# Attention with relation maps: both sides of a unit in one ring of four map buffers, logarithm and inverse for two maps at a time, three units ahead

## The chip, the core and the metric

One core of a Trainium2 chip runs the whole kernel in one launch. The metric is the time of one execution on the device in microseconds (us). Before the change the median of three runs was 4457.25 us (4456.81 to 4464.74). The engines are TensorE (PE; PEld is its weight load), VectorE (DVE), ScalarE (ACT), GpSimd (POOL) and SyncE (SP), which issues most of the DMAs. Each runs its own instructions in order and meets the others through semaphores.

## What is computed

A pre-norm block over 4096 tokens of width 256: attention with 16 heads, and a mixture of 8 experts of which each token takes two. The change lies in the attention alone:

```python
x = hidden_states                       # layer-normed, 1 x 4096 x 256
q, k, v = (x @ W.T + b, split in 16 heads of 16)
attn_scores = einsum('bihd,bjhd->bhij', q, k) / scale
li = x @ rel_W[:, :d].T
lj = x @ rel_W[:, d:].T
logits = li[:, :, None, :] + lj[:, None, :, :] + rel_b      # 3 classes for each pair of tokens
relation_probs = softmax(logits, axis=-1)
bias = einsum('bijk,hk->bhij', relation_probs, logical_bias)
gate = sigmoid(x @ gate_W.T + gate_b)
attn_scores = attn_scores + gate * bias
out = softmax(attn_scores) @ v          # for each head
```

For each pair (query i, key j) three relation probabilities are needed. With the differences of the logits, d0 and d1, two of them follow from r = 1 / (1 + exp(d0) + exp(d1)) and its like: that is what a *map* holds here.

## The kernel before

Three stages follow one another: the projections (to about 188 us), the attention (`attend`, from there to about 3600 us) and the experts. Only `attend` changes.

**Chunks and steps.** The 4096 queries are taken in 32 chunks of 128. The first 24 chunks run in a loop on the chip of three turns with eight chunks each (`in_chunks`), the last eight stand behind it without a loop. A chunk goes over 32 key tiles of 128 keys, `jt` = 0 to 31; I call one of them a *step*. In a step PE does, in this order (L814 products, L802 relation, L833 maxima, L856 values):

- the scores of the *next* step, `pe_scores(jt + 1)`: 16 relation matmuls for the even heads, 16 for the odd heads, 32 products of queries and keys on top of them in the same two halves of the PSUM tensor `sc`. Each half may be overwritten only after ACT has read it, so the relation matmuls of a half wait for the exponentials of this step (`p_ready`);
- a pair of maximum matmuls (`pe_step_pair`, slot 0) for the row maxima of the next chunks;
- `pe_pv(jt)`: 16 matmuls, exponentials times values, into `acc`, when both exponentials of this step are done;
- a second pair of maximum matmuls (slot 1).

ACT does the two exponentials of the step's scores (L690) and then a piece of work on a relation map. DVE does four maximum reductions (L716), one for each maximum matmul, out of a ring of three PSUM banks (`mx`), and between the third and the fourth one *clamp* (L708, `dve_d`): the logit difference of a query row and 512 keys, capped at 43, for one of the two differences.

**Maps.** A *unit* is 512 keys, four steps; a chunk has 8 units. A unit has two maps, side 0 (the first 64 queries of the chunk) and side 1 (the others), on 128 partitions each, so 16 maps in a chunk, numbered `g`, with unit `u = g // 2`. The life of a map before the change:

1. DVE clamps both halves of it into `dl` (side, half), one in each step, `D_AHEAD` = 3 steps of clamping ahead of ACT's counting;
2. ACT exponentiates both halves at once, 1024 elements a row, from `dl` into `ex` (L668; even steps, `act_r_exp`);
3. POOL adds the two halves (L613);
4. ACT takes the logarithm of 1 + sum (L675) and the exponential of its negative (L677), 512 elements a row, in the next, odd step (`act_r_inv`);
5. POOL rounds the result to 16 bits (`rhi`, L623) and keeps the rest (`rlo`, L625);
6. SP sends both by six DMAs per unit into `rst`, the operand of the relation matmuls, which holds two units.

`ex` is a ring of two maps, `dl` another of two. The map worked on in step `jt` is `g = jt // 2 + R_AHEAD`, four maps (two units) ahead of the unit that PE uses. The order on each engine is written out by hand.

**Prologue of the stage.** PE and DVE go over 64 pairs of maxima for chunk 0 and 16 for chunk 1; during the first eight pairs DVE clamps the first four maps. SP meanwhile loads the key logits `dj`, eight DMAs of 512 KB (unit 0 and 1 count on semaphore `dj_in0`, units 2 to 7 on `dj_in1`), and behind them in its queue a store to `attention_out`. DVE waits for `dj_in1` after all pairs.

## Time and profile before

| what | value |
|---|---|
| median of three runs | 4457.25 us (4456.81 to 4464.74) |
| the profiled execution: its own time | 4429.6 us |
| its span, and granted TensorE clock | 4427.9 us, 0.943 |
| PE, PEld busy | 3634.5 us (82%), 2679.5 us (61%) |
| DVE busy | 3607.0 us (81%) |
| ACT busy | 3309.5 us (75%) |
| POOL busy | 1970.2 us (44%) |
| first score exponential of chunk 0 | at 341.52 us |
| last ones of chunk 31 | at 3594.52 us |

The span is cut by the page into 40 slices of 110.7 us, one digit each for the busy tenths:

```profile
PE   7548888888888888888888888989888864499991
DVE  4298999999899999998999999999999623377773
ACT  2008999999899999998999999999999941244440
POOL 0014444454444455544455454555555532533335
PEclk9759999999999999999999999999999986699996
```

Slices 4 to 33 are the attention's chunks. Busy shares of 80 to 90% on three engines at once say that they wait for one another in turn; what a piece of work is worth has to be read from the order in which they meet. Times of instructions below are in microseconds from the start of the span unless ns is written. Instructions of one engine overlap a little (the next one starts up to 0.1 us before the last ends), so the distance between starts is what counts for a sum.

### The profile page before, as it was taken

What the parts mean: (1) busy time and instruction counts of PE and PEld (TensorE: products, weight loads), DVE (VectorE), ACT (ScalarE), POOL (GpSimd) and SP (SyncE); (2) the same over time, 40 slices, a digit from 0 to 9 for tenths busy, and PEclk for the clock granted to TensorE, in tenths of its full rate; (3) what the DMA queues carried; (4) which work ended last, traced back from release to release, by engine and by line L of the source; (5) the groups of instructions that cost most, each with busy time, mean ns of one, the idle gap of its engine ahead of it and who ended that gap; (6) DMA issues with size and microseconds to landing.
All of it is one profiled execution on the core that took longest, in us unless ns stands there. A gap on an engine that the chain in (4) does not pass through costs nothing. (4 is left out here: it accounts for less than half of the span.)

```text
span 4427.9 us, 243862 instructions
## 1 busy us (share of the span) xinstructions
PE 3634.5 (82%) x106896; PEld 2679.5 (61%) x106896; DVE 3607.0 (81%) x6310; ACT 3309.5 (75%) x3946; POOL 1970.2 (44%) x1816
## 2 busy tenths in 40 slices
PE   7548888888888888888888888989888864499991
PEld 4306666666666666666666666666666654377771
DVE  4298999999899999998999999999999623377773
ACT  2008999999899999998999999999999941244440
POOL 0014444454444455544455454555555532533335
PEclk9759999999999999999999999999999986699996
DMA  5412222222222222222222222222222252344433
GB/s 106 75 41 65 71 69 71 70 73 70 66 72 66 72 68 73 70 66 69 71 71 71 71 71 71 73 68 77 71 71 74 70 180 87 123 150 152 154 123 123
DMA packets 368338, 371.66 MB, mean 84 GB/s; under 512 B 108416, under 2 KB 342272, under 8 KB 363296
## 3 DMA queue, kind: packets, MB, share of 16 engines
q1 hardware_dynamic: 358080, 338.08, 28.0%
q8 instruction: 857, 14.04, 1.3%
q0 software_dynamic: 6144, 16.79, 1.2%
q14 instruction: 217, 1.78, 0.1%
q10 hardware_dynamic: 3040, 0.98, 0.1%
HBM read 99.58 MB, written 46.40 MB: 33 GB/s over the span
## 5 line engine op out<-in xcount | busy, mean ns | idle before, releaser
L716 DVE TENSOR_REDUCE b_mxp<-b_mx 128x1 f32<-128x512 f32 x4096 | 2641.2, 683 | 221.6 <-PE b_mx L833 185.1
L690 ACT ACTIVATE b_pr<-b_sc 128x1024 f32<-128x1024 f32 x2048 | 1980.1, 1019 | 319.2 <-PE b_sc L814 302.2
L856 PE MATMUL b_acc<-b_pr,vp 128*32 128x128 f32 x32768 | 1161.1, 276 | 30.6 <-issue 26.3
L856 PEld LDWEIGHTS b_acc<-b_pr,vp 128*32 128x32 f32 x32768 | 851.7, 109 | 302.7 <-issue 295.6
L802 PE MATMUL b_sc<-b_cm,b_rst 64*128 64x64 f16 x32768 | 808.9, 191 | 236.2 <-ACT b_pr L690 148.2
L833 PE MATMUL b_mx<-kst,b_qt 64*128 64x512 f16 x4096 | 818.7, 392 | 172.5 <-DVE b_mxp L716 151.3
L802 PEld LDWEIGHTS b_sc<-b_cm,b_rst 64*128 64x128 f16 x32768 | 670.2, 95 | 453.1 <-ACT b_pr L690 240.5
L613 POOL TENSOR_TENSOR b_ex<-b_ex 128x512 f32<-128x512 f32 x512 | 657.2, 1284 | 561.3 <-ACT b_ex L668 551.2
L623 POOL CAST b_rhi<-b_ex 128x512 f16<-128x512 f32 x512 | 316.5, 618 | 1069.0 <-ACT b_ex L677 764.0
L814 PE MATMUL b_sc<-b_qt,kst 64*128 64x64 f16 x32768 | 693.0, 191 | 64.5 <-issue 61.0
L814 PEld LDWEIGHTS b_sc<-b_qt,kst 64*128 64x128 f16 x32768 | 573.9, 95 | 86.8 <-issue 83.3
L625 POOL TENSOR_TENSOR b_rlo<-b_ex,b_rhi 128x512 f16<-128x512 f32 x512 | 594.4, 1161 | 40.9
L708 DVE TENSOR_SCALAR b_dl<-b_dj,b_const 128x512 f32<-128x512 f32 x1024 | 520.5, 510 | 68.4 <-ACT b_ex L668 40.3
L668 ACT ACTIVATE b_ex<-b_dl 128x1024 f32<-128x1024 f32 x512 | 541.6, 1058 | 36.8 <-DVE b_dl L708 36.8
L833 PEld LDWEIGHTS b_mx<-kst,b_qt 64*128 64x128 f16 x4096 | 201.8, 94 | 430.9 <-DVE b_mxp L716 389.4
L677 ACT ACTIVATE b_ex<-b_ex 128x512 f32<-128x512 f32 x512 | 322.8, 630 | 16.2
L1315 ACT ACTIVATE c_h<-c_ps,c_b1b 128x512 f32<-128x512 f32 x184 | 126.6, 689 | 276.6 <-PE c_ps L1348 229.4
L675 ACT ACTIVATE b_ex<-b_ex 128x512 f32<-128x512 f32 x512 | 323.5, 632 | 8.6 <-POOL b_ex L613 8.6
L1348 PE MATMUL c_ps<-c_xT,c_w1p 128*128 128x512 f16 x1104 | 258.3, 385 | 10.0 <-DVE c_xT L1185 9.9
L1359 PE MATMUL c_ps<-c_w2p,c_a 128*128 128x256 f16 x2208 | 255.4, 273 | 0.0
L1359 PEld LDWEIGHTS c_ps<-c_w2p,c_a 128*128 128x128 f16 x2208 | 216.0, 98 | 36.0
L1194 DVE TENSOR_TENSOR c_a<-c_h,c_a 128x512 f16<-128x512 f32 x184 | 210.3, 1143 | 6.3
(144 smaller groups left out, 1623.1 us busy)
## 6 DMA issues: line engine op xcount, KB each, us to landing
b_rst<-b_rhi SPq DMA_DIRECT2D x1024, 128.0 KB
b_rst<-b_rlo SPq DMA_DIRECT2D x512, 128.0 KB
c_w1r<-in_L_ffn_W_dram SPq DMA_DIRECT2D x23, 1024.0 KB, 4.9
c_w2r<-in_L_ffn_W_dram SPq DMA_DIRECT2D x23, 1024.0 KB, 4.9
expert_tokens<-c_zeros SPq DMA_DIRECT2D x23, 512.0 KB, 6.7
c_xb<-expert_tokens SPq DMA_DIRECT2D x23, 512.0 KB
expert_results<-c_y SPq DMA_DIRECT2D x23, 512.0 KB, 2.8
b_qt<-q_parts SPq DMA_DIRECT2D x64, 128.0 KB
```

What stands on the lines that cost most here:

```text
L613: nc.gpsimd.tensor_tensor(ex[:, g % 2, 0], ex[:, g % 2, 0], ex[:, g % 2, 1], ALU.add).then_inc(s["sum_ready"], 1)
L625: nc.gpsimd.tensor_tensor(rlo[:, slot], ex[:, g % 2, 0], rhi[:, slot], ALU.subtract).then_inc(s["lo_ready"], 1)
L668: nc.scalar.activation(ex[:, k].rearrange("p n j -> p (n j)"), dl[:, k].rearrange("p n j -> p (n j)"), ACT.Exp).then_inc(s["e_ready"], 1)
L675: nc.scalar.activation(ex[:, k, 0], ex[:, k, 0], ACT.Ln, bias=1.0).then_inc(s["ln_ready"], 1)
L690: nc.scalar.activation(pr[:, jt % 2, half, :], sc[:, half].rearrange("p a b -> p (a b)"), ACT.Exp).then_inc(s["p_ready"], 1)
L708: nc.vector.tensor_scalar(dl[:, side, n], dj[:, u, n], const[:, par, side, n:n + 1], EXP_MAX, ALU.add, ALU.min).then_inc(s["d_ready"], 1)
L716: nc.vector.tensor_reduce(mxp[:, head, part:part + 1], mx[:, (bank + ab) % MX_RING, :], AX.X, ALU.max).then_inc(s["mx_used"], 1)
L802: ins = pe.matmul(out, rst[rows, u % 2, b, j0:j0 + P], cm[rows, par, half, b], start=(b == 0), stop=False, skip_group_check=True)
L814: ins = pe.matmul(sc[:, ab, side, pair * IS:pair * IS + IS], kst[rows, pair, jt * P:jt * P + P], qt[rows, slot4, pair, side * IS:side * IS ...
L833: pe.matmul(mx[:, (bank + ab) % MX_RING, :], qt[rows, slot4, pair, :], kst[rows, pair, j0:j0 + 512], start=True, stop=True).then_inc(s["mx ...
L856: ins = pe.matmul(acc[32 * (h % 4):32 * (h % 4) + 32, h // 4, :], vp[:, jt, VW * h:VW * h + 32], pr[:, jt % 2, h % 2].rearrange("p (a h i) ...
L1359: ins = pe.matmul(ps[:, 4 + d % 2, 0:D], hT[:, b % 2, hp, f, t * P:t * P + P], w2p[:, b % 2, wp, f, :], start=(f == 0 and hp == 0 and wp = ...
```

## The change

`dl` is gone. DVE clamps straight into `ex`, now a ring of four maps, and ACT exponentiates in place. A clamp waits until POOL's subtraction of the map four before is done (`lo_ready`) where it waited for ACT's exponential of the map two before. ACT's four steps of a unit now are: exponential of side 0, exponential of side 1, logarithm of both maps, inverse of both maps (`act_r_step`). The logarithm and the inverse are one instruction each over 2 x 512 elements a row. ACT works three units ahead (`U_AHEAD`), and the clamps count from map 6 on, still with `D_AHEAD` = 3. POOL adds both sides first, then rounds and subtracts both sides; the two multiplications that make the gate operand `cm` stand together in unit 6. In the prologue six maps are clamped, at pairs 0, 2, 4, 6, 24 and 28 (`MAP_AT`); the wait for `dj_in1` stands ahead of the fifth.

```diff
-R_AHEAD, D_AHEAD = 4, 3
+U_AHEAD, D_AHEAD, MAPS = 3, 3, 4
+MAP_AT = (0, 2, 4, 6, 24, 28)
-C_MAPS = (13, 14)
+C_UNIT = 6
...
-        dl = sb("dl", [P, 2, 2, JU])
-        ex = sb("ex", [P, 2, 2, JU])
+        ex = sb("ex", [P, MAPS, 2, JU])
...
         def pool_parts(pool, x, g):
             u, n = g // 2, 16 * x + g
-            pool.wait_ge(s["r_ready"], n + 1)
+            pool.wait_ge(s["r_ready"], UNITS * x + u + 1)
...
-                for turn in range(2 * UNITS):
-                    g = turn + R_AHEAD
-                    if g < 2 * UNITS:
-                        pool_sum(pool, c, g)
...
+                for w in range(UNITS):
+                    u = w + U_AHEAD
+                    for side in range(2):
+                        if u < UNITS:
+                            pool_sum(pool, c, 2 * u + side)
...
+                    for side in range(2):
+                        if u < UNITS:
+                            pool_parts(pool, c, 2 * u + side)
...
+        def act_r_exp(act, x, g):
+            act.wait_ge(s["d_ready"], 2 * (16 * x + g) + 2)
+            both = ex[:, g % MAPS].rearrange("p n j -> p (n j)")
+            nc.scalar.activation(both, both, ACT.Exp).then_inc(s["e_ready"], 1)
+        def act_r_ln(act, x, u):
+            both = ex[:, 2 * (u % 2):2 * (u % 2) + 2, 0]
+            act.wait_ge(s["sum_ready"], 16 * x + 2 * u + 2)
+            nc.scalar.activation(both, both, ACT.Ln, bias=1.0).then_inc(s["ln_ready"], 1)
+        def act_r_inv(act, x, u):
+            both = ex[:, 2 * (u % 2):2 * (u % 2) + 2, 0]
+            act.wait_ge(s["ln_ready"], UNITS * x + u + 1)
+            nc.scalar.activation(both, both, ACT.Exp, scale=-1.0).then_inc(s["r_ready"], 1)
+        def act_r_step(act, x, u, step):
+            if step < 2:
+                act_r_exp(act, x, 2 * u + step)
+            elif step == 2:
+                act_r_ln(act, x, u)
+            else:
+                act_r_inv(act, x, u)
...
-                    g = jt // 2 + R_AHEAD
-                    if g < 2 * UNITS:
-                        (act_r_inv if jt % 2 else act_r_exp)(act, c, g)
+                    u = jt // 4 + U_AHEAD
+                    if u < UNITS:
+                        act_r_step(act, c, u, jt % 4)
...
-            if n == 0 and not (isinstance(x, int) and x == 0 and g < 2):
-                dve.wait_ge(s["e_ready"], 16 * x + g - 1)
-            nc.vector.tensor_scalar(dl[:, side, n], dj[:, u, n], const[:, par, side, n:n + 1], EXP_MAX, ALU.add,
+            if n == 0 and not (isinstance(x, int) and x == 0 and g < MAPS):
+                dve.wait_ge(s["lo_ready"], 16 * x + g - MAPS + 1)
+            nc.vector.tensor_scalar(ex[:, g % MAPS, n], dj[:, u, n], const[:, par, side, n:n + 1], EXP_MAX, ALU.add,
...
             for n in range(PAIRN):
-                if n % 2 == 0 and n < 2 * R_AHEAD:
+                if n in MAP_AT:
+                    if MAP_AT.index(n) == MAPS:
+                        dve.wait_ge(s["dj_in1"], 16 * (UNITS - 2))
                     for k in range(2):
-                        dve_d(dve, 0, 0, 1, n // 2, k)
+                        dve_d(dve, 0, 0, 1, MAP_AT.index(n), k)
...
-            dve.wait_ge(s["dj_in1"], 16 * (UNITS - 2))
             for n in range(D_AHEAD):
-                dve_d(dve, 0, 0, 1, R_AHEAD + n // 2, n % 2)
+                dve_d(dve, 0, 0, 1, 2 * U_AHEAD + n // 2, n % 2)
...
-                                g, k = R_AHEAD + (jt + D_AHEAD) // 2, (jt + D_AHEAD) % 2
+                                g, k = 2 * U_AHEAD + (jt + D_AHEAD) // 2, (jt + D_AHEAD) % 2
```

How the instructions stand on ACT in one of the last eight chunks, with what each waits for; before the change (`b_pr` are the exponentials of scores, `b_ex` the maps, `b_dl` the clamped logits):

```order
L690 ACTIVATE b_pr<-b_sc 128x1024 [waits b_scores_ready] x2
L668 ACTIVATE b_ex<-b_dl 128x1024 [waits b_lo_ready,b_d_ready]
L690 ACTIVATE b_pr<-b_sc 128x1024 [waits b_scores_ready] x2
L675 ACTIVATE b_ex<-b_ex 128x512 [waits b_sum_ready]
L677 ACTIVATE b_ex<-b_ex 128x512 [waits b_ln_ready]
```

and now:

```order
L705 ACTIVATE b_pr<-b_sc 128x1024 [waits b_scores_ready] x2
L671 ACTIVATE b_ex<-b_ex 128x1024 [waits b_d_ready]
L705 ACTIVATE b_pr<-b_sc 128x1024 [waits b_scores_ready] x2
L671 ACTIVATE b_ex<-b_ex 128x1024 [waits b_d_ready]
L705 ACTIVATE b_pr<-b_sc 128x1024 [waits b_scores_ready] x2
L677 ACTIVATE b_ex<-b_ex 128x2x512 [waits b_sum_ready]
L705 ACTIVATE b_pr<-b_sc 128x1024 [waits b_scores_ready] x2
L683 ACTIVATE b_ex<-b_ex 128x2x512 [waits b_ln_ready]
```

Before, two steps made one map; now four steps make two, with the two map exponentials in steps that follow each other. DVE still does one clamp in every step, so the clamps are spaced evenly while the exponentials that read them are not.

On DVE the prologue reads, before the change (`b_mxp` are the maximum reductions):

```order
L708 TENSOR_SCALAR b_dl<-b_dj,b_const 128x512 x2
L716 TENSOR_REDUCE b_mxp<-b_mx 128x1 x116
L722 TENSOR_REDUCE b_mrow<-b_mxp 128x16
L726 SCALAR_TENSOR_TENSOR b_m<-b_mrow,b_bound 128x16
L716 TENSOR_REDUCE b_mxp<-b_mx 128x1 x32
L708 TENSOR_SCALAR b_dl<-b_dj,b_const 128x512 x3
```

and now:

```order
L723 TENSOR_SCALAR b_ex<-b_dj,b_const 128x512 x2
L731 TENSOR_REDUCE b_mxp<-b_mx 128x1 x36
L723 TENSOR_SCALAR b_ex<-b_dj,b_const 128x512 x2
L731 TENSOR_REDUCE b_mxp<-b_mx 128x1 x8
L723 TENSOR_SCALAR b_ex<-b_dj,b_const 128x512 x2
L731 TENSOR_REDUCE b_mxp<-b_mx 128x1 x72
L737 TENSOR_REDUCE b_mrow<-b_mxp 128x16
L741 SCALAR_TENSOR_TENSOR b_m<-b_mrow,b_bound 128x16
L731 TENSOR_REDUCE b_mxp<-b_mx 128x1 x32
L723 TENSOR_SCALAR b_ex<-b_dj,b_const 128x512 x3
```

The 116 reductions behind the fourth map are cut into 36, 8 and 72 by the clamps of the fifth and sixth map, whose key logits belong to unit 2.

On POOL, in the last chunks, before the change (`b_rhi` is the rounding, `b_rlo` the subtraction):

```order
L613 TENSOR_TENSOR b_ex<-b_ex 128x512 [waits b_e_ready]
L623 CAST b_rhi<-b_ex 128x512 [waits b_r_ready,b_r_in1]
L625 TENSOR_TENSOR b_rlo<-b_ex,b_rhi 128x512 [waits b_hi_ready]
L613 TENSOR_TENSOR b_ex<-b_ex 128x512 [waits b_e_ready]
L623 CAST b_rhi<-b_ex 128x512 [waits b_r_ready,b_r_in0]
```

and now:

```order
L613 TENSOR_TENSOR b_ex<-b_ex 128x512 [waits b_e_ready] x2
L623 CAST b_rhi<-b_ex 128x512 [waits b_r_ready,b_r_in0]
L625 TENSOR_TENSOR b_rlo<-b_ex,b_rhi 128x512 [waits b_hi_ready]
L623 CAST b_rhi<-b_ex 128x512 [waits b_r_ready,b_r_in0]
L625 TENSOR_TENSOR b_rlo<-b_ex,b_rhi 128x512 [waits b_hi_ready]
```

Rounding and subtraction of the two sides stand directly behind one another, where a sum stood between them.

## Rows read from the trace of the kernel before

**Rows 1.** Groups by line, 1000 to 3000 us: count | busy us, mean ns | idle before

```profile
L690 ACT ACTIVATE b_pr<-b_sc 128x1024 f32<-128x1024 f32 x1248 | 1206.8, 1019 | 145.5 <-PE b_sc L814 133.4 <-issue 4.2
L668 ACT ACTIVATE b_ex<-b_dl 128x1024 f32<-128x1024 f32 x312 | 330.1, 1058 | 0.0
...
L677 ACT ACTIVATE b_ex<-b_ex 128x512 f32<-128x512 f32 x312 | 196.7, 630 | 9.9
...
L716 DVE TENSOR_REDUCE b_mxp<-b_mx 128x1 f32<-128x512 f32 x2497 | 1610.9, 683 | 149.0 <-PE b_mx L833 130.6
```

**Rows 2.** Timeline, ACT, the last steps (start, us, what, [idle before])

```profile
3577.08 1.94 ACT L690 ACTIVATE b_pr<-b_sc 128x1024 f32<-128x1024 f32 x2 [0.97 <-PE b_sc L814]
```

**Rows 3.** Timelines of ACT, PE and DVE, steps 4 to 6 of chunk 16

```profile
2008.62 1.92 ACT L690 ACTIVATE b_pr<-b_sc 128x1024 f32<-128x1024 f32 x2
2010.42 1.06 ACT L668 ACTIVATE b_ex<-b_dl 128x1024 f32<-128x1024 f32 x1
2011.50 1.94 ACT L690 ACTIVATE b_pr<-b_sc 128x1024 f32<-128x1024 f32 x2
2013.33 0.63 ACT L675 ACTIVATE b_ex<-b_ex 128x512 f32<-128x512 f32 x1
...
2014.53 1.92 ACT L690 ACTIVATE b_pr<-b_sc 128x1024 f32<-128x1024 f32 x2
...
2010.83 0.64 PE L814 MATMUL b_sc<-b_qt,kst 64*128 64x64 f16 x32
...
2011.61 1.08 PE L856 MATMUL b_acc<-b_pr,vp 128*32 128x128 f32 x32
2012.63 0.39 PE L833 MATMUL b_mx<-kst,b_qt 64*128 64x512 f16 x2
...
2011.04 2.70 DVE L716 TENSOR_REDUCE b_mxp<-b_mx 128x1 f32<-128x512 f32 x4
2013.66 0.48 DVE L708 TENSOR_SCALAR b_dl<-b_dj,b_const 128x512 f32<-128x512 f32 x1
```

**Rows 4.** Timelines of DVE and ACT, later units of that chunk: clamp, next-but-one exponentials

```profile
2027.04 0.48 DVE L708 TENSOR_SCALAR b_dl<-b_dj,b_const 128x512 f32<-128x512 f32 x1
...
2039.86 0.48 DVE L708 TENSOR_SCALAR b_dl<-b_dj,b_const 128x512 f32<-128x512 f32 x1
...
2052.57 0.48 DVE L708 TENSOR_SCALAR b_dl<-b_dj,b_const 128x512 f32<-128x512 f32 x1
...
2065.13 0.48 DVE L708 TENSOR_SCALAR b_dl<-b_dj,b_const 128x512 f32<-128x512 f32 x1
...
2027.49 1.92 ACT L690 ACTIVATE b_pr<-b_sc 128x1024 f32<-128x1024 f32 x2
...
2040.68 1.92 ACT L690 ACTIVATE b_pr<-b_sc 128x1024 f32<-128x1024 f32 x2
...
2054.09 1.94 ACT L690 ACTIVATE b_pr<-b_sc 128x1024 f32<-128x1024 f32 x2 [0.58 <-PE b_sc L814]
...
2066.15 1.94 ACT L690 ACTIVATE b_pr<-b_sc 128x1024 f32<-128x1024 f32 x2
```

**Rows 5.** Prologue: DVE and SP timelines, landing of `attention_out`, windows (last: GB/s)

```profile
225.07 0.88 DVE L708 TENSOR_SCALAR b_dl<-b_dj,b_const 128x512 f32<-128x512 f32 x2 [27.97 <-DMA b_dj<-key_logits]
...
237.99 80.52 DVE L716 TENSOR_REDUCE b_mxp<-b_mx 128x1 f32<-128x512 f32 x116
...
216.69 50.15 SPq L502 DMA_DIRECT2D b_dj<-key_logits x6
...
DMA to landing us min/median/max: 24.4/24.4/24.4
...
245.00:265.00 20.00, 8.51 (x28) 1.46 (x28) 18.57 (x29) 0.00 (x0) 0.68 (x1) 0.50 0.13 53
```

**Rows 6.** Timelines of POOL and DVE: a cast (L623) and a clamp (L708)

```profile
2001.11 0.61 POOL L623 CAST b_rhi<-b_ex 128x512 f16<-128x512 f32 x1 [7.42 <-ACT b_ex L677]
...
2001.21 0.80 DVE L708 TENSOR_SCALAR b_dl<-b_dj,b_const 128x512 f32<-128x512 f32 x1
```

More of the change, by code:

```diff
@@ L638, in _ @@
             pool.wait_ge(s["eye_made"], len(first_rows) + 1)
-            for g in range(R_AHEAD):
-                pool_sum(pool, 0, g)
-                pool_parts(pool, 0, g)
+            for u in range(U_AHEAD):
+                for side in range(2):
+                    pool_sum(pool, 0, 2 * u + side)
+                for side in range(2):
+                    pool_parts(pool, 0, 2 * u + side)
             for half in range(2):
@@ L659, in _ @@
[L659 to L677 removed]
+                for w in range(UNITS):
+                    u = w + U_AHEAD
+                    for side in range(2):
+                        if u < UNITS:
+                            pool_sum(pool, c, 2 * u + side)
+                        elif not last:
+                            pool_sum(pool, c + 1, 2 * (u - UNITS) + side)
+                    if w == C_UNIT and not last:
+                        for half in range(2):
+                            pool_c(pool, c + 1, 1 - par, nth + par, half)
+                    for side in range(2):
+                        if u < UNITS:
+                            pool_parts(pool, c, 2 * u + side)
+                        elif not last:
+                            pool_parts(pool, c + 1, 2 * (u - UNITS) + side)
@@ L681, in _ @@
             nc.scalar.preload_act_table_set("natural_log_exp_and_others")
-            for g in range(R_AHEAD):
-                act_r_exp(act, 0, g)
-                act_r_inv(act, 0, g)
+            for u in range(U_AHEAD):
+                for step in range(4):
+                    act_r_step(act, 0, u, step)
             def chunk(c, par, nth, last, slot4):
```

31 lines of the change are left out of this document (5 added, 26 removed).

## The prediction

> **What bounds the kernel now.** First I read the page's 40 slices: 30 of them are the attention stage, in which VectorE (DVE) and ScalarE (ACT) are both at nine tenths and TensorE (PE) at eight; so no engine's sum alone tells the price of an edit. Then the groups by line of a long stretch of that stage. A key tile (a "step") costs ACT two score exponentials of 1.02 us, and in turn either one 1058 ns map exponential (even steps) or a logarithm and an inverse of 630 ns each (odd steps) [rows 1]. 312 map exponentials in 2000 us are 624 steps of 3.205 us; four steps, one "unit" of the change, take 12.8 us. ACT is idle 145.5 us there, 0.93 us per unit, nearly all of it waiting for scores [rows 1].
>
> The timeline of one undisturbed piece shows why [rows 3]. Score exponentials start at 2008.62, 2011.50 and 2014.53: an even step takes 2.88 us, an odd one 3.03 us. After the second exponential (ends 2010.4) PE does the second half of the relation matmuls and the products (2010.83 to 2011.47), and ACT starts the next scores at 2011.50; the map exponential fits just into that gap (2010.42 to 2011.48). The pair logarithm, inverse needs 2013.33 to 14.53 = 1.20 us, so there ACT itself is last. That PE's way alone needs as long as an even step is seen in the last steps of the stage, where no map is left to do: 1.94 us of exponentials and 0.97 us of waiting, 2.91 us [rows 2]. So a step can't go under about 2.9 us, whatever ACT saves.
>
> DVE matters by its order. In step k it reduces three maximum banks, does one clamp (L708, which the map exponential reads), and reduces the fourth. The third reduction needs the pair of matmuls that PE issues after step k's attention-times-value product, and that product needs step k's exponentials: exponentials of step 4 of a chunk at 2008.62, product at 2011.61, pair at 2012.63, clamp at 2013.66, done at 14.14 [rows 3]. The clamp of a step thus ends 5.5 us after its exponentials start, which is 0.8 us after ACT reaches the map work of the *next* step (2013.33). Before the change this hurts nobody, since a map's second clamp is done two steps ahead of its exponential.
>
> **The change, part by part.**
>
> *Logarithm and inverse for two maps.* 512 pairs of 630 ns become 256 pairs of instructions over 1024 elements a row. No row shows a logarithm of that size; the map exponential of the same size takes 1058 ns, twice the small one 1260. I take the nearer shape, 1058, and keep 1260 as the upper end. Steps 2 and 3 of a unit then look like an even step. Start to start that is 1.08 us (2010.42 to 2011.50) against 1.20: 0.12 us less for an odd step where ACT is last. The other odd step of the unit is priced below. ACT's idle time is 0.23 us a step [rows 1], more than that saving, so part of the steps gain nothing: I take two thirds, -0.08 us per unit, bounds 0 and -0.12.
>
> *The map exponential of side 1 moves to step 1.* Counted out of the code: at key tile jt DVE clamps half (jt+3) mod 2 of map 6+(jt+3)//2, and ACT at jt = 4(u-3)+1 exponentiates map 2u+1. Its second clamp is issued at jt = 4(u-3), one step before; side 0 keeps two steps. So once per unit ACT, in order, stands at the map exponential until a clamp that cannot be early, and behind it in ACT's queue are the score exponentials of the next step, for which PE, and behind PE DVE, wait. Price: clamp end + 0.04 + 1.08 against the start that the next scores had. In the piece above 2014.14+1.12 = 2015.26 against 2014.53: +0.73 us. The next four units of that chunk give 2027.52+1.12 against 2027.49, 2040.34+1.12 against 2040.68, 2053.05+1.12 against 2054.09 and 2065.61+1.12 against 2066.15 [rows 4]: +1.15, +0.78, +0.08, +0.58. Mean +0.66 us per unit. This step was an odd one, so its shorter or longer map work is already in it.
>
> *Ring of four, in place.* The clamp now waits until POOL's subtraction of the map four before has read the slot. The inverse of unit u ends in step 4u-9 and both sides' cast and subtraction take 2 x 1.8 us after it; the clamps that need the slots stand in steps 4u-7 and 4u-5, over 3 us later each. No cost. Dropping the wait of the map exponential for that subtraction: nothing, ACT never stood there. Reading and writing the same place: 630 ns is already an in-place row; nothing. Side slots and DMAs of the relation rows: as many and at the same steps as before, with their data a unit earlier, so SP waits less; nothing.
>
> *POOL in another order.* Sums of both sides first, then cast, subtraction, cast, subtraction in one piece of 3.7 us after the inverse of step 3. The clamp of step 3 comes 5.0 to 5.5 us into that step, the second cast too. A clamp that starts 0.10 us after a cast took 0.80 us instead of 0.48 [rows 6]: it ended 0.28 us after the cast. I take half of the units hit by 0.32 us, and two thirds of that carried on to the next clamp, on which ACT waits: +0.1 us per unit; below 0 it cannot be; if the clamp falls behind a whole subtraction it is about +0.7, which is the upper end. The Trainium skill (SBUF — State Buffer, Who interferes with whom) says that a tensor_scalar in its two-port mode and a GpSimd instruction lock each other out for the whole instruction, whoever starts first; rows 6 agree with it, and it speaks against this change, because the piece on POOL is now twice as long. By that rule, with a clamp behind a whole subtraction in every unit, the sum would be rival 3's; by the rows it is +0.1 us.
>
> Sum of the loop: 0.66 - 0.08 + 0.1 = 0.68 us per unit, 256 units: +174 us.
>
> *The prologue.* Maps 4 and 5 are now clamped at n = 24 and 28 of DVE's 64 pairs, and ahead of map 4 DVE waits for all six late key-logit loads. Before, that wait stood after everything. DVE begins its 116 reductions after map 3 at 237.99, 0.694 us each; 36 of them bring it to 263.0 [rows 5]. The last of the six loads is issued in a row of issues that ends at 266.84, and the store queued behind them lands 24.4 us after 266.9, so they have landed by 291.3 at the latest; the queue moves 53 GB/s, that is 9.9 us for 512 KB, and the first two let DVE go at 225.07: 225 + 6 x 9.9 + 5 for the query tiles = 290 [rows 5]. The wait is 27 us (at least 266.8 + 9.9 - 263 = 13, at most 28). The reductions behind it are what the prologue is made of, so nothing hides it. Four more clamps there, 0.8 us a pair: +1.6; as many fewer behind the last unit, where nothing waits for them. Together +29 us.
>
> **Sum.** 174 + 29 = +203 us on the profiled execution's 4429.6 us: 4633. The median shown is 4457.25, 27.7 us above that execution; I carry that over: 4660 us.
>
> **Rivals.**
> 1. *The wait is half paid back.* While ACT stands, PE and DVE catch up, and stalls that cost ACT 0.93 us per unit [rows 1] vanish in it. For it: undisturbed steps of 2.88 and 2.91 would make a unit 3 x 2.9 + 3.75 = 12.45 us against 12.8. Against: ACT's waits fall in single steps by PE's own delays, and only those in the delayed step are covered. Half of 0.93: +0.22 per unit, +55, with the prologue 4541.
> 2. *The other side: all of it is paid back.* The delayed step resets the phase of the three engines, every other step runs at 2.9, and a unit costs 12.45 + 0.2 for the end of a chunk = 12.65, which is 0.17 less than now: -44 + 29 = -15 us, 4442. It decides once stalls outside the delayed step fall below 0.25 us a unit. Rows 4 speak against it: in that chunk the gaps between the exponentials vary from 2.9 to over 3.5 us with no long wait before them.
> 3. *DVE behind POOL.* The clamp of step 3, or the critical one of the next unit, falls into a subtraction: +0.45 per unit more, +115, 4775.
> 4. *The change doesn't do what it says:* the two-map logarithm costs twice the small one. The unit's steps 2 and 3 get 0.2 longer each where ACT is last: +70, 4730.
>
> **How the numbers follow.** Forecast (wait each unit and prologue, 4600 to 4715): 0.68. Rival 1, 4480 to 4600: 0.15. Rival 2: 0.06. Rivals 3 and 4: 0.09 together. 0.02 for what I don't see. The range leaves out rival 2, the lower third of rival 1 and the upper part of 3: 4520 to 4725. About 0.2% (9 us) can be told from no change. Faster comes from rival 2 alone, 0.04; same 0.03, from between rivals 2 and 1; slower 0.93.
>
> **What would show it.** Right: ACT's map exponential waits for the clamp some 256 times, 0.7 to 1.3 us each, nearly all on side 1; three steps of a unit at 2.9 us and one at 3.7 or more; DVE idle 27 us near 263 us before a clamp, on a DMA; two-map logarithm and inverse near 1.06 us; no longer waits for scores than before. Wrong: no idle time before the map exponential; the first scores still near 342 us; a wait of DVE for POOL's subtraction; a unit under 12.8 us.

## Result and the profile after

The change made the kernel slower: median 4546.9 us (4534.88 to 4554.93, 4 runs) against 4460.36 us (4456.81 to 4464.74, 4 runs), ratio 1.0198 with a 95% interval of 1.0182 to 1.0215, so +87 us. I had forecast 4660, +203 us. The sign, the two places and the order of events are as forecast; the size is under half (0.43).

The first reading is by stage. Below are the windows of the changed kernel (stretch and its length, busy time and instructions of PE, PEld, DVE, ACT and POOL, granted clock, DMA share, GB/s), cut at the start of the attention stage, at its first score exponential and after its last:

```profile
188.00:372.00 184.00, 50.37 (x224) 10.23 (x224) 116.53 (x178) 13.98 (x14) 23.94 (x39) 0.51 0.09 31
372.00:3724.00 3352.00, 2849.98 (x102304) 2095.91 (x102304) 3014.92 (x5105) 2942.14 (x3060) 1603.20 (x1580) 1.00 0.26 68
```

The kernel before has 153.5 us and 3256.5 us there, and the stretches ahead of and behind the attention are the same to 1 us. So the prologue grew by 30 us (forecast 29), and the chunks by 95 by these two profiles. The first profile of before, however, lay below all of its timed runs. From the first score exponentials of chunk 0 to the last of chunk 31 it has 3253 us, the changed kernel 3348 us, and a second profile of before (below) 3286 us. Against the second one the chunks grew by 62 us; with the prologue's 30 that makes 92, for 87 us between the medians.

The prologue, by the timelines of DVE and ACT:

```profile
237.81 24.88 DVE L731 TENSOR_REDUCE b_mxp<-b_mx 128x1 f32<-128x512 f32 x36
292.03 0.88 DVE L723 TENSOR_SCALAR b_ex<-b_dj,b_const 128x512 f32<-128x512 f32 x2 [29.34 <-DMA b_dj<-key_logits]
...
371.87 1.94 ACT L705 ACTIVATE b_pr<-b_sc 128x1024 f32<-128x1024 f32 x2 [68.19 <-PE b_sc L830]
```

DVE reaches the fifth map after 36 reductions at 262.7 us and stands for 29.3 us until the key logits are there, at the place and about the length worked out from [rows 5].

The chunks, by line, 1000 to 3000 us (the rows that answer to [rows 1]):

```profile
L705 ACT ACTIVATE b_pr<-b_sc 128x1024 f32<-128x1024 f32 x1209 | 1169.2, 1019 | 68.5 <-PE b_sc L830 58.5
L671 ACT ACTIVATE b_ex<-b_ex 128x1024 f32<-128x1024 f32 x302 | 319.5, 1058 | 187.9 <-DVE b_ex L723 187.9
L677 ACT ACTIVATE b_ex<-b_ex 128x1024 f32<-128x1024 f32 x152 | 160.7, 1057 | 0.0
L683 ACT ACTIVATE b_ex<-b_ex 128x1024 f32<-128x1024 f32 x151 | 159.9, 1059 | 0.0
...
L723 DVE TENSOR_SCALAR b_ex<-b_dj,b_const 128x512 f32<-128x512 f32 x604 | 339.0, 561 | 0.0
```

302 map exponentials in 2000 us are 151 units of 13.24 us. ACT stands 187.9 / 151 = 1.24 us in each before a map exponential, waiting for the clamp: the new wait. But its wait for scores fell from 0.93 us a unit to 68.5 / 151 = 0.45, and logarithm and inverse of two maps take 1058 ns, as assumed. The clamp's mean rose to 561 ns.

One unit, by the timelines of ACT, DVE and POOL; the rows answer to [rows 3]:

```profile
2099.55 1.94 ACT L705 ACTIVATE b_pr<-b_sc 128x1024 f32<-128x1024 f32 x2
2103.01 1.06 ACT L671 ACTIVATE b_ex<-b_ex 128x1024 f32<-128x1024 f32 x1 [1.52 <-DVE b_ex L723]
2103.97 1.92 ACT L705 ACTIVATE b_pr<-b_sc 128x1024 f32<-128x1024 f32 x2
...
2106.86 1.94 ACT L705 ACTIVATE b_pr<-b_sc 128x1024 f32<-128x1024 f32 x2
...
2109.77 1.94 ACT L705 ACTIVATE b_pr<-b_sc 128x1024 f32<-128x1024 f32 x2
...
2098.84 1.34 DVE L723 TENSOR_SCALAR b_ex<-b_dj,b_const 128x512 f32<-128x512 f32 x1
...
2102.50 0.47 DVE L723 TENSOR_SCALAR b_ex<-b_dj,b_const 128x512 f32<-128x512 f32 x1
...
2098.05 0.62 POOL L623 CAST b_rhi<-b_ex 128x512 f16<-128x512 f32 x1
2098.74 1.16 POOL L625 TENSOR_TENSOR b_rlo<-b_ex,b_rhi 128x512 f16<-128x512 f32 x1
```

Step 1 starts at 2099.55 and takes 4.42 us, since the map exponential waits 1.52 us for the clamp that ends at 2102.97; the next two steps take 2.89 and 2.91 us with no wait at all. The clamp at 2098.84 starts inside POOL's subtraction (2098.74 to 2099.90) and takes 1.34 us; four reductions follow it without a pause, and then the critical clamp, which is late for that reason.

Taken over the starts of the score exponentials of the first 252 units (all but the last four), a unit's steps 0 to 3 last on average:

| kernel | step 0 | 1 | 2 | 3 | sum |
|---|---|---|---|---|---|
| before, first profile | 3.12 | 3.26 | 3.14 | 3.21 | 12.73 |
| before, second profile | 3.17 | 3.26 | 3.19 | 3.25 | 12.86 |
| changed | 3.11 | 4.08 | 2.92 | 3.00 | 13.11 |

Step 1 costs 0.82 us more, which is the forecast's 0.66 and 0.1 for POOL. Steps 2 and 3 cost 0.43 to 0.52 us less together, where the forecast had 0.08. That is where most of the missing 116 us are.

The same traces say what the shorter steps are made of. ACT's idle time ahead of the score exponentials, sorted by the step that it stands before, in us per unit, 1000 to 3000 us:

| kernel | before step 0 | 1 | 2 | 3 | sum |
|---|---|---|---|---|---|
| before, second profile | 0.22 | 0.33 | 0.20 | 0.36 | 1.11 |
| changed | 0.13 | 0.26 | 0.00 | 0.06 | 0.45 |

A wait before a step lengthens the step ahead of it. So the wait at the end of the delayed step 1 (0.20) is gone. That at the end of step 2 has lost 0.30 us, as much as step 2 became shorter. That at the end of step 3 has lost 0.09, and up to 0.12 us more of step 3 is the shorter map work. The experiments ask whether this is a rule.

### The profile page after: what moved, and what is told of

Its sections match the earlier page's. It is cut to its first block and busy times, and to the rows that moved or that the text cites. A ratio compares the mean times of both kernels' runs of the same rounds, so it can differ in the third digit from the quotient of the medians.

```text
span 4553.1 us, 243035 instructions
## 1 busy us (share of the span) xinstructions
PE 3628.9 (80%) x106896; PEld 2658.7 (58%) x106896; DVE 3676.8 (81%) x6310; ACT 3238.0 (71%) x3434; POOL 1960.6 (43%) x1816
## 5 line engine op out<-in xcount | busy, mean ns | idle before, releaser
L872 PE MATMUL b_acc<-b_pr,vp 128*32 128x128 f32 x32768 | 1140.7, 276 | 19.2 <-issue 16.9
L818 PEld LDWEIGHTS b_sc<-b_cm,b_rst 64*128 64x128 f16 x32768 | 656.6, 95 | 604.9 <-ACT b_pr L705 449.2
L671 ACT ACTIVATE b_ex<-b_ex 128x1024 f32<-128x1024 f32 x512 | 541.7, 1058 | 391.2 <-DVE b_ex L723 391.2
L623 POOL CAST b_rhi<-b_ex 128x512 f16<-128x512 f32 x512 | 313.8, 613 | 1084.5 <-ACT b_ex L683 1075.3
L830 PE MATMUL b_sc<-b_qt,kst 64*128 64x64 f16 x32768 | 678.6, 191 | 32.8 <-issue 30.2
L723 DVE TENSOR_SCALAR b_ex<-b_dj,b_const 128x512 f32<-128x512 f32 x1024 | 578.6, 567 | 86.6 <-DMA b_dj<-key_logits 58.1
L625 POOL TENSOR_TENSOR b_rlo<-b_ex,b_rhi 128x512 f16<-128x512 f32 x512 | 607.8, 1187 | 40.9
L677 ACT ACTIVATE b_ex<-b_ex 128x1024 f32<-128x1024 f32 x256 | 270.6, 1057 | 5.1 <-POOL b_ex L613 5.1
L683 ACT ACTIVATE b_ex<-b_ex 128x1024 f32<-128x1024 f32 x256 | 271.1, 1059 | 0.1
```

The costliest lines, as they stand in the source:

```text
L625: nc.gpsimd.tensor_tensor(rlo[:, slot], ex[:, slot, 0], rhi[:, slot], ALU.subtract).then_inc(s["lo_ready"], 1)
L671: nc.scalar.activation(both, both, ACT.Exp).then_inc(s["e_ready"], 1)
L723: nc.vector.tensor_scalar(ex[:, g % MAPS, n], dj[:, u, n], const[:, par, side, n:n + 1], EXP_MAX, ALU.add, ALU.min).then_inc(s["d_ready"], 1)
L818: ins = pe.matmul(out, rst[rows, u % 2, b, j0:j0 + P], cm[rows, par, half, b], start=(b == 0), stop=False, skip_group_check=True)
L830: ins = pe.matmul(sc[:, ab, side, pair * IS:pair * IS + IS], kst[rows, pair, jt * P:jt * P + P], qt[rows, slot4, pair, side * IS:side * IS ...
L872: ins = pe.matmul(acc[32 * (h % 4):32 * (h % 4) + 32, h // 4, :], vp[:, jt, VW * h:VW * h + 32], pr[:, jt % 2, h % 2].rearrange("p (a h i) ...
```

## Experiments

Theory A: a delay of ACT is largely paid back, because ACT would have waited for PE in the same and the next steps anyway. Theory B: each wait counts in full, and the shorter steps 2 and 3 are the gain of the batching. The runs come in groups, each with runs of the kernel before on the same chip; the median of before differs from group to group (4435 to 4492 us), so kernels are compared by the ratio to it. "Loop" is the mean step of the 24 chunks in the loop on the chip, "rest" that of the first 60 units of the eight chunks behind it. "Both" is the changed kernel with the edits of the first two experiments.

| run | edit | median us | ratio (95%) | loop | rest |
|---|---|---|---|---|---|
| (before, two profiles) | | 4460.4 | 1 | 3.21, 3.26 | 3.09, 3.08 |
| (changed) | | 4546.9 | 1.0198 (1.0182-1.0215) | 3.31 | 3.17 |
| e1_late_maps | maps 4, 5 late | 4510.8 | 1.0143 (1.0126-1.0160) | 3.30 | 3.15 |
| e2_clamps_4_ahead | clamps 4 ahead | 4511.8 | 1.0147 (1.0119-1.0175) | 3.29 | 3.06 |
| e3_both | e1 and e2 | 4484.2 | 1.0074 (1.0055-1.0093) | 3.29 | 3.07 |
| e4_clamp_slot_0 | clamp earlier in the step | 4509.1 | 1.0137 (1.0121-1.0154) | 3.26 | 3.16 |
| e5_before_clamps_2_ahead | before, two waits a unit | 4560.9 | 1.0220 (1.0194-1.0245) | 3.32 | 3.26 |
| e6_before_act_063 | before, ACT work | 4485.7 | 1.0049 (1.0029-1.0069) | 3.26 | 3.14 |
| e7_both_split_ln | both, no batching | 4478.1 | 1.0091 (1.0066-1.0115) | 3.27 | 3.07 |
| e8_pool_sides_apart | both, POOL's pieces apart | 4496.8 | 1.0075 (1.0050-1.0100) | 3.29 | 3.11 |
| e9_before_pe_dose | before, 16 small matmuls | 4860.3 | 1.0953 (1.0925-1.0982) | 3.66 | 3.43 |
| e10_before_dve_dose | before, DVE work | 4487.8 | 1.0111 (1.0082-1.0139) | 3.29 | 3.11 |
| e11_both_short_sub | both, short subtraction | 4440.9 | 1.0006 (0.9993-1.0020) | 3.23 | 3.08 |
| e12_before_pe_long | before, 1 long matmul | 4507.2 | 1.0078 (1.0053-1.0104) | 3.31 | 3.11 |
| e13_after_short_sub | changed, short subtraction | 4522.7 | 1.0109 (1.0092-1.0126) | 3.28 | 3.14 |
| e14_before_unrolled | before, no loop | 4320.9 | 0.9662 (0.9646-0.9678) | 3.07 | 3.07 |
| e15_both_unrolled | both, no loop | 4317.2 | 0.9658 (0.9642-0.9674) | 3.08 | 3.05 |
| e16_after_unrolled | changed, no loop | 4456.4 | 0.9921 (0.9899-0.9943) | 3.19 | 3.16 |
| e17_act_063_unrolled | e6, no loop | 4390.4 | 0.9777 (0.9755-0.9799) | 3.14 | 3.12 |

**The prologue and the wait, undone.**

```diff
-MAP_AT = (0, 2, 4, 6, 24, 28)
+MAP_AT = (0, 2, 4, 6, 56, 60)      # e1, e3
-U_AHEAD, D_AHEAD, MAPS = 3, 3, 4
+U_AHEAD, D_AHEAD, MAPS = 3, 4, 4   # e2, e3
-CLAMP_SLOT, ACC_SLOT = 1, 0
+CLAMP_SLOT, ACC_SLOT = 0, 0        # e4
```

> Maps 4 and 5 of the prologue are clamped at pairs 56 and 60 in place of 24 and 28; all else as in the changed kernel. DVE reaches pair 56 at about 263 + 64 x 0.694 = 307 us, after the last key logits have landed (they released DVE at 292 us). If the 29 us wait of DVE in the prologue is the whole cost of the prologue (30.3 us between the first score exponentials of the two kernels), this run is 27 to 30 us under the changed kernel's 4547: 4518, and the first score exponential is back at 342 to 344 us. Rival: the stage's start is set by something else too (POOL's work on maps 4 and 5 now comes late, the gate operand stands behind it in POOL's queue, and PE waits for that operand): then it gains less than 20 us.

e1 starts its first score exponentials at 344.1 us for 371.9, 27.8 us earlier, and is 0.55% (25 us) under the changed kernel. So nearly all of the prologue's cost is the wait for the key logits.

> Clamps one step earlier (D_AHEAD 4 for 3), all else as in the changed kernel: both clamps of side 1 are now done two steps before the exponential that reads them. Theory A (a wait is only partly lost): the 1.22 us that ACT stands before each map exponential of side 1 goes, but the steps 2 and 3 of a unit, which ran at 2.92 and 3.00 us with the wait, go back to about 3.12 as the steps of the kernel before; a unit 4 x 3.12 = 12.48 against 13.11: -160 us, 4387. Theory B (waits are lost in full and the shorter steps come from batching alone): steps 2 and 3 stay at 2.92 and 3.00, step 1 falls to about 3.0: unit 12.0, -280 us, 4265. Theory C (the clamps are not what ACT waits for): no change.

> Both edits: clamps four steps ahead, and maps 4 and 5 late in the prologue. If the two costs are apart, the gains add: by theory A 4547 - 160 - 29 = 4358, by theory B 4238. Either would beat the kernel before (4460).

> The clamp of a step stands between the first and second reduction instead of the third and fourth; distance in steps unchanged (3). If the clamp is late because it is queued behind the reduction that needs PE's attention-times-value product, it now ends about 2 x 0.61 us earlier and no longer behind that product: 5.5 - 1.9 = 3.6 to 4.3 us after the exponentials of its step start, before ACT needs it at 4.7. The wait of ACT goes from 1.22 us a unit to under 0.3, and the time goes as with clamps four ahead, within 40 us. Rival: DVE's backlog, not PE's product, makes the clamp late: it then gains only the 0.6 to 1.2 us of the shifted place in units where DVE lags, and half of the wait stays: 4460 to 4500.

The waits of ACT in e2, and then in e4, with e4's clamp:

```profile
L705 ACT ACTIVATE b_pr<-b_sc 128x1024 f32<-128x1024 f32 x1222 | 1184.3, 1021 | 241.5 <-PE b_sc L830 233.5
L671 ACT ACTIVATE b_ex<-b_ex 128x1024 f32<-128x1024 f32 x306 | 324.0, 1059 | 0.0
```

```profile
L705 ACT ACTIVATE b_pr<-b_sc 128x1024 f32<-128x1024 f32 x1227 | 1188.4, 1020 | 168.8 <-PE b_sc L830 155.0
L671 ACT ACTIVATE b_ex<-b_ex 128x1024 f32<-128x1024 f32 x307 | 324.8, 1058 | 59.2 <-DVE b_ex L723 57.6 <-issue 0.8
...
L723 DVE TENSOR_SCALAR b_ex<-b_dj,b_const 128x512 f32<-128x512 f32 x613 | 444.3, 725 | 0.0
```

The new wait is gone in e2, all of it, and the kernel gains 0.5% (23 us), not the 160 or 280 us that the two theories gave: ACT now waits 241.5 us for scores where it waited 68.5. e3 adds the two gains and is still 0.7% slower than the kernel before, although ACT has less to do in it. In e4 most of the wait goes too (59.2 for 187.9 us); the clamp now meets POOL's work more often (725 ns), and the gain is 0.6% (27 us), about that of e2, as its forecast said (the wait left is 0.39 us a unit, where under 0.3 was expected). Since e2 gains no more without any wait, the longer clamp is not what keeps the gain of e4 small. The forecasts of e2 and e3 missed in the same way: something other than ACT's wait holds these kernels at 3.26 to 3.31 us a step in the loop.

**What a delay of ACT costs by itself.** In the kernel before:

```diff
-R_AHEAD, D_AHEAD = 4, 3
+R_AHEAD, D_AHEAD = 4, 2                                              # e5
+                    if jt % 4 == 1:                                   # e6, e17
+                        nc.scalar.activation(junk[:, :], dj[:, 0, 0], ACT.Exp)
```

> The kernel before, profiled once more. Its first profile lay at 4429.6 us, below every one of its timed runs so far (4442 to 4465). If that profile was a low one, this one has its chunks (first to last score exponential) longer than the 3253 us of the first, by 10 to 30 us, with projections, prologue and experts the same to 1 us; if the profiled execution is always shorter than the timed ones, it lies near 4430 again.

It lay at 4459.85 us with 3286 us of chunks: the first profile was a low one, not a rule.

> The kernel before with its clamps one step later (D_AHEAD 2 for 3), so that both maps of a unit, not one, have their second clamp one step ahead of the exponential. By the clamp arithmetic ACT stands about 0.9 us or more before every map exponential, 512 times. Theory A (a wait is about half paid back by the steps behind it): 512 x 0.7 x 0.5 = +180 us over before, 4630. Theory B (in full): 512 x 0.75 = +380 us, 4830. If DVE's backlog also shrinks, less than A.

> The kernel before with one extra ACT instruction in every fourth step (after logarithm and inverse, 128 x 512, about 0.63 us, its result unused): 256 x 0.55 to 0.63 us = 141 to 161 us more work for ACT and nothing else. It asks what one delay per unit costs by itself. Theory B (every delay of ACT counts in full): +140 to +160 over before, 4590 to 4605. Theory A (the steps behind it run at their floor, as steps 2 and 3 did in the changed kernel at 2.92 and 3.00 in place of 3.14 and 3.21): 0.6 - 0.35 = 0.25 us a unit, +65 us, 4510; the delayed step is 3.8 to 3.9 us, the next two under 3.0 and 3.07.

ACT in the second profile of before, in e5 and in e6, 1000 to 3000 us:

```profile
L690 ACT ACTIVATE b_pr<-b_sc 128x1024 f32<-128x1024 f32 x1230 | 1189.7, 1019 | 170.6 <-PE b_sc L814 158.8 <-issue 4.7
```

```profile
L690 ACT ACTIVATE b_pr<-b_sc 128x1024 f32<-128x1024 f32 x1205 | 1156.1, 1010 | 17.8 <-PE b_sc L814 13.0 <-issue 4.4
L668 ACT ACTIVATE b_ex<-b_dl 128x1024 f32<-128x1024 f32 x301 | 318.2, 1057 | 207.9 <-DVE b_dl L708 207.3 <-issue 0.6
```

```profile
L691 ACT ACTIVATE b_pr<-b_sc 128x1024 f32<-128x1024 f32 x1230 | 1188.1, 1017 | 99.4 <-PE b_sc L817 87.3 <-issue 4.3
...
L699 ACT ACTIVATE b_junk<-b_dj 128x512 f16<-128x512 f32 x154 | 94.4, 613 | 0.0
```

e6 is the plain case: 256 instructions of 613 ns, 157 us of work, cost 0.49% (0.29 to 0.69%), that is 22 us, a seventh. ACT's wait for scores falls from 170.6 to 99.4 us in the stretch, which pays for 71 of the 94.4 us. In e5 ACT waits 207.9 us for clamps and almost no more for scores (17.8 for 170.6): the two waits of a unit are 207.9 / 150.5 = 1.38 us, 354 us in all, and cost 98 us. Both came out under theory A's own numbers (65 and 180 us); theory B is ruled out.

**The batching.** e7 undoes it in "both": one logarithm and one inverse instruction per map again.

> The kernel with both edits, with logarithm and inverse again as one instruction per map (four of 630 ns for two of 1058 ns in a unit): it undoes the batching alone. ACT gets 0.24 us more work a unit. If work of ACT costs little in the loop chunks and counts in the last eight chunks (as in the run with the extra instruction: 0.003 and 0.05 us a step for 0.15), this costs 0 in the loop and up to 0.05 us a step in the rest: +5 to +15 us, 4490 to 4500. If the batching is worth what it saves on ACT: +60 us, 4545.

The medians are 4478.1 and, in another group, 4484.2 us; the ratios are 1.0091 and 1.0074 with intervals that overlap. The difference is +8 us, give or take 14: the batching is worth nothing measurable here, and at most some 20 us, which leaves room for the forecast 5 to 15 but not for 60.

**POOL and the clamp.**

```diff
# e8: side 1's cast and subtraction one unit later in POOL's order
+            if late:
+                pool.wait_ge(s["ln_ready"], UNITS * x + u + 2)
...
+                    pool_parts(pool, c, 2 * (u - 1) + 1, True)
+                    pool_parts(pool, c, 2 * u)
# e11 (both), e13 (changed): rlo zeroed once, then
-            nc.gpsimd.tensor_tensor(rlo[:, slot], ex[:, slot, 0], rhi[:, slot], ALU.subtract)
+            nc.gpsimd.tensor_tensor(rlo[:, slot, 0:32], ex[:, slot, 0, 0:32], rhi[:, slot, 0:32], ALU.subtract)
```

> The kernel with both edits (clamps four ahead, maps 4 and 5 late in the prologue; 4484 us) and POOL's cast and subtraction of side 1 put off until the logarithm of the next unit is done, so that POOL has one piece of at most 1.9 us in each step. Theory P (with the wait gone, what holds that kernel at 3.24 us a step is DVE: its clamps take 620 ns on average against 489 before because they start inside POOL's longer pieces): the clamp falls to 480 to 510 ns, 0.12 us less DVE work a step, the loop chunks from 3.27 to about 3.15 us a step: -100 us, 4385, faster than the kernel before. Rival Q (the clamp's length is hidden; PE's instruction supply holds the steps): the clamp gets shorter and the time stays within 15 us of 4484. Side effect to watch: DVE may wait for side 1's subtraction, which now ends about when the clamp wants its slot.

> The kernel with both edits (4484 us), with POOL's subtraction over 32 of 512 columns; the rest of the low parts stays zero, so the scores lose their low parts there. It takes some 0.95 us per map out of POOL's pieces, so that DVE's clamps meet POOL seldom: clamp from 620 to about 520 ns. If the longer clamps (0.12 us a step over the kernel before) are why that kernel's loop chunks run at 3.29 us a step in place of 3.21 to 3.26, they go back to 3.2: -50 to -90 us, 4395 to 4435. If the clamps' length is hidden, under 15 us.

> The changed kernel with POOL's subtraction over 32 of 512 columns (low parts of the scores' bias stay zero elsewhere). The clamp of step 3 took 812 ns on average in place of 478, and the maximum's last step 1117 ns against 493; both meet POOL's piece. If that is handed on to the clamp that ACT waits for, the wait falls from 1.24 us a unit to about 0.95 and the kernel gains 0.3 x 256 = 75 us in full or, paid back in part as the other delays, 20 to 50: 4500 to 4525. If it is hidden, under 10.

The clamp in e8 (with its new wait) and in e11:

```profile
L729 DVE TENSOR_SCALAR b_ex<-b_dj,b_const 128x512 f32<-128x512 f32 x610 | 343.3, 563 | 16.3 <-POOL b_rlo L627 16.3
```

```profile
L724 DVE TENSOR_SCALAR b_ex<-b_dj,b_const 128x512 f32<-128x512 f32 x620 | 332.8, 537 | 0.0
```

e8 shortened the clamp from 620 to 563 ns and gained nothing, so my ordering was no cure (it lays the casts and sums into other clamps, and DVE waits 16 us for POOL). The short subtraction does gain: 0.7% (30 us, for 50 to 90 forecast) in e11, 0.9% (40 us, within the 20 to 50 forecast) in e13, where ACT's wait falls from 1.24 to 1.02 us a unit. So the subtraction costs the changed kernel about 0.15 us a unit. How much of that the kernel before pays as well is not known, since it was not run with the short subtraction; the forecast's 0.1 was a difference to it. And since both runs also shorten POOL's own chain, not only the clamps, this is the price of the subtraction in POOL's order, not of the clamp's length alone.

**What holds the loop chunks.**

```diff
-            for b in range(NB):
+            for b in (0, 0, 0, 0, *range(NB)):                  # e9: relation matmuls
...
+                        if slot == 0:                            # e10
+                            nc.vector.tensor_reduce(junk[:, jt:jt + 1], dj[:, 0, 0, 0:128], AX.X, ALU.max)
...
+                for _ in range(2 if again and ab == 0 else 1):   # e12: maximum matmul of slot 0
                     ins = pe.matmul(mx[:, (bank + ab) % MX_RING, :], qt[rows, slot4, pair, :],
...
-    with eng.Fori(0, LOOPS) as turn:                             # e14 to e17
-        for n in range(UNROLL):
-            chunk(turn * UNROLL + n, n % 2, turn * (UNROLL // 2) + n // 2 + 1, False, n % QR)
-    for c in range(LOOPS * UNROLL, NT):
+    for c in range(NT):
         chunk(c, c % 2, c // 2 + 1, c == NT - 1, c % QR)
```

> The kernel before, with the first two relation matmuls of each half issued four more times (they start the accumulation anew, so nothing changes in the result): 16 of 84 matmuls more in a step, 0.24 us of PE by the start-to-start time of the relation matmuls (16 in 0.24 us), 0.12 of it between ACT's second exponential and the next scores. Theory S (the loop chunks, at 3.21 to 3.31 us a step in all eight kernels so far, are held by PE and its instructions, which is why 0.61 us more of ACT work per unit cost the loop chunks 0.003 us a step): nearly all of 0.24 us counts, +200 to +300 us over before, 4660 to 4750. Theory T (the three engines share the bound): +0.12 us a step, +120 us, 4580.

> The kernel before, with one more reduction of 128 x 128 in each step on DVE ahead of its first (result unused), about 0.2 us start to start. Under theory S DVE has as much room as ACT in the loop chunks: less than +60 us over before. If instead DVE is what holds the loop chunks (it is busy 0.90 of them), nearly all counts: +150 to +200 us, 4610 to 4660.

> The kernel before, with the first maximum matmul of the pair in slot 0 issued twice (64 x 512, the second overwrites the first with the same): one matmul and one weight load more a step, about 0.2 us of PE time, outside the stretch between ACT's second exponential and the next scores. Against e9 (32 instructions more a step, 0.24 us: +0.42 us a step in the loop chunks). If PE's time as such holds the loop chunks: +0.2 us a step, +200 us, 4640. If it is the supply of PE's instructions: 2 more of some 200 instructions, +1% of a step and whatever PE's slack doesn't cover: under +60 us, below 4495.

PE's waits on nothing that the profile shows ("issue"), ahead of the relation matmuls (in total, times, longest), before (second profile), in e9 and in the changed kernel:

```profile
PE b_sc L802 <- issue: 54.6, 88, 4.7
```

```profile
PE b_sc L802 <- issue: 120.6, 177, 3.8
```

```profile
PE b_sc L818 <- issue: 28.8, 39, 4.0
```

The answers to a dose differ by engine: 0.15 us a step on ACT costs 0.02, some 0.2 on DVE costs 0.05 (1.1%, 50 us), 0.24 on PE in 16 small matmuls costs 0.42 us (9.5%, 425 us, for 200 to 300 forecast), more than its own time. One long matmul a step, some 0.2 us of PE in two instructions, costs 0.78%, 35 us. Of the four, only many more instructions of PE cost more than their time. One thing keeps e9 and e12 from being a clean pair: half of e9's matmuls lie between ACT's second exponential and the next scores, and e12's does not.

The traces tell more about the "issue" waits than these lines do. I count all of PE's instructions in the order of the trace (matmuls, weight loads and the sequencer's own; some 205 a step in the loop, 201 outside it) and take PE's waits of this kind over 0.2 us, 1000 to 3000 us. From one to the next it is a multiple of 256 instructions, to within three, in 219 of 223 cases in the second profile of before, in 435 of 437 in e9 and in 83 of 83 in e14; by chance it would be one in 37. There are 224 such waits before, in 493 blocks of 256 instructions, 438 in e9 (507 blocks), 105 in the changed kernel, 21 in e5 and 84 in e14. In e9, from one such wait to the wait 256 instructions on, it takes a median of 3.9 us. So PE stands at the edges of blocks of 256 of its instructions. That the next block is not there yet is the reading that fits; no run shows the delivery itself. It fits the repaid wait too: where PE waits longer for ACT (161.9 us ahead of the relation matmuls in the changed kernel, 76.3 before), it stands less often at such an edge.

> The kernel before with all 32 chunks written out, no loop on the chip; waits have constants and the register instructions in front of them go. The last eight chunks, which are written so, run at 3.08 us a step against 3.21 to 3.26 of the loop chunks. If the register instructions (or the loop's turns) make that difference: 768 steps x 0.15 = -115 us and the two loop turns (some 10 us) less: 4330 to 4345. If the last chunks are faster for another reason (no work for chunks behind them), nothing.

> The kernel with both edits (clamps four ahead, maps 4 and 5 late in the prologue), all chunks written out. Its last eight chunks run at 3.07 us a step: 1024 x 3.07 = 3145 us of chunks in place of 3312, 4320. If ACT is last in some steps once PE's supply is no longer short, the two-map logarithm and inverse count now, and this kernel is 5 to 20 us under the written-out kernel before; if not, the longer clamps make it equal or slower.

> The changed kernel with all chunks written out, to be held against the written-out kernel before (4321 us, 0.9662 of before). If the shortage of PE instructions in the loop paid the wait back, the change costs more here: the prologue's 30 us and most of the forecast 0.68 us per unit, 4321 + 30 + 150 = 4500. If slack of the three engines pays back by itself, the cost is that of the last eight chunks, 3.16 to 3.17 us a step against 3.08: 30 + 1024 x 0.09 = +120, 4443.

> The written-out kernel before with the extra ACT instruction of 0.61 us in every fourth step (157 us in all). In the looped kernel it cost 22 us. The last eight chunks showed +0.05 us a step for it: 1024 x 0.054 = +55 us over the written-out kernel, 4376, if slack as such absorbs the rest; +100 us or more, 4420, if it was the shortage alone that absorbed it.

ACT's waits in e14, and then in e16, 1000 to 3000 us:

```profile
L687 ACT ACTIVATE b_pr<-b_sc 128x1024 f32<-128x1024 f32 x1300 | 1255.3, 1017 | 77.8 <-PE b_sc L811 69.5
```

```profile
L702 ACT ACTIVATE b_pr<-b_sc 128x1024 f32<-128x1024 f32 x1256 | 1214.2, 1018 | 34.0 <-PE b_sc L827 21.5
L668 ACT ACTIVATE b_ex<-b_ex 128x1024 f32<-128x1024 f32 x314 | 332.4, 1058 | 156.7 <-DVE b_ex L720 156.7
```

Written out, the kernel before takes 0.9662 of its time, 151 us less (forecast 115 to 125), and all its chunks run at the 3.07 us a step of the last eight; ACT's wait for scores is more than halved (77.8 for 170.6 us), and PE's unexplained wait ahead of the relation matmuls, 54.6 us in the loop, is 15.2:

```profile
PE b_sc L799 <- issue: 15.2, 30, 1.3
```

"Both" written out is level with it (0.9658), though its clamps still take 570 ns for 488. These two are the fastest versions of the study and beat both kernels. The change costs 0.9921 - 0.9662 = 2.6% here against 2.0% in the loop, and the extra ACT work 1.15% (51 us, a third of its 157) against 0.49%. So what the loop adds paid back part of the wait, but less than half: with the prologue's 30 us, wait and prologue come to 286 us here (1.00 us a unit) and cost 115, and to 348 us in the loop (1.24 us a unit) and cost 87. The larger part is paid back with or without the loop. Both of the last two came out near the lower of their two forecasts.

## Why the prediction was wrong

**Point by point.** The prologue: right, 30 us for 29, with a wait of 29.3 us for 27. The second clamp of side 1 ends after ACT wants it: right; step 1 takes 0.82 us more, for 0.76 forecast with POOL's term. Two-map logarithm near 1.06 us: right. Ring of four and DMAs at no cost: right, DVE does not wait for the subtraction. POOL's piece: right in kind. The clamp was hit (over 0.6 us) in 116 of 150 units, where I had taken half, and was 0.34 us longer on average; the short subtraction takes 0.22 us of ACT's wait and about 0.15 us of time off a unit, for 0.1 forecast, but the kernel before was not run with it. No longer waits for scores than before: right, and that is the point I did not follow up.

**The step that failed** is the sum over a unit: "I take two thirds, -0.08 us per unit, bounds 0 and -0.12" for all that steps 2 and 3 give back. They gave back 0.27 and 0.25 us (against the second profile). Only 0.12 us in one of them can be the batching, and in e7 that has no measurable worth; the rest is ACT's wait for scores, which went from 1.1 us a unit (170.6 / 154) to 0.45; nearly 0.4 us of that lie at the ends of steps 2 and 3. I had priced the wait against the start that the next scores had in five units, added it up as if the steps behind kept their own waits, and put the case in which they do not (rival 1, half paid back, 4541 us) at 0.15. It was the case that came: 4547. The lower bound of that term should have been all of the 0.93 us of waits shown in [rows 1]. e6 shows the repayment with nothing else changed (0.61 us of work a unit, 0.46 us less waiting for scores), and e5 with the wait itself.

**A second, smaller point** is that the sum was worked out on a low execution and its growth carried over to the median with the 27.7 us. The first profile was low in its chunks, 3253 against 3286 us in the second, and it had fewer waits for scores, 0.93 against 1.11 us a unit. The waits that can be paid back were thus taken too small as well. The first profile and that of the changed kernel differ by 125 us, the medians by 87.

**What stays open.** That PE's "issue" waits stand at blocks of 256 instructions is shown, the delivery behind them is not. Writing out the chunks removes the register instructions of all five engines and the loop's turns at once. The traces part the two: at each of the two turns the eight steps around it take about 8 us more than those around the other ends of chunks (34.2 and 34.9 for 26.7 us in the second profile), 16 of the 141 us by which the 24 chunks became shorter. The other 125 us are 0.16 us in every step; which engine's register instructions they come from was not tried. Why "both", with less work on ACT and no wait for clamps, is still 0.7% slower than before in the loop is not shown either. The short subtraction takes it back to 1.0006, but the kernel before was not run with it; e8, which parted POOL's long piece, gained nothing; and written out, the two are level.

## What to carry to other kernels

Where three engines wait for one another in turn, a new wait on one of them costs at least what it is longer than the waits that this engine already has in the same and the next steps; add those up first, the difference is the lower bound. Here the cost lay a little above it: in e5 256 x (1.38 - 1.11) = 69 us by the rule and 98 measured, in e6 nothing by the rule and 22 measured. Before work on an engine is cut, add some to it: 157 us more on ACT for 22 us told, in one run, that batching its instructions could win little, and 16 small matmuls pointed to PE's instructions. When an instruction is moved one step, count for its reader and its producer in which step each stands: even spacing on one side and pairs on the other made one clamp in four late.

## What the runs showed of the hardware

- The same kernel, with its loop of three turns of eight chunks written out, takes 3.4% less time (0.9662, 0.9646 to 0.9678), at 3.07 us a step for 3.21 to 3.26. Each of the two turns of the loop costs 7 to 8 us (6.6 in the changed kernel).
- 16 matmuls of 64 x 64 f16 more in a step of 84, each with its weight load, 15 ns from start to start in a burst, cost 0.40 to 0.44 us a step in the loop and about 0.35 outside it, not 0.24.
- PE's waits of over 0.2 us without a releaser stand a multiple of 256 of its instructions apart: 219 of 223 distances before, 435 of 437 in e9, 83 of 83 in e14.
- A clamp (DVE, 128 x 512 f32, SBUF to SBUF, one input, 0.48 us alone) that starts while a POOL instruction has more than 0.15 us to go ends about 0.28 us after it: all 226 of them in the changed kernel end 0.27 to 0.33 us after it, and they take up to 1.50 us. One that starts less than 0.06 us ahead of POOL's is mostly held as well (16 of 21). One that starts 0.06 to 0.2 us ahead takes its usual time (19 of 19 before), and POOL's instruction is then the longer one: a cast takes 0.82 for 0.61 us. That agrees with the lock that the Trainium skill (SBUF — State Buffer, Who interferes with whom) describes.
- The median of the kernel before lay between 4435 and 4492 us (1.3%) in groups of runs on five chips, and all of the difference between two profiles of it (33 us) lay in the chunks.
